# Dilated attention on one core: another order of the steps on TensorE, ScalarE and VectorE, and the maximum's high part on VectorE

## The chip, the cores and the metric

The kernel runs on one core of one Trainium2 chip, as one launch. The metric is the device time of that launch in microseconds (us). A core has five engines that run their own queues of instructions and meet at semaphores: TensorE (PE in the profile; its weight loads are PEld), VectorE (DVE), ScalarE (ACT), GpSimd (POOL) and SyncE (SP), which here issues most transfers.

## The reference

Four stages, each followed by a layer norm of the sum with its input: dilated attention, a mixture of 8 experts, linear attention, and a soft mixture with slots. Only the first is touched:

```python
D_MODEL, NUM_HEADS, HEAD_DIM, DILATION, SEGMENT = 256, 16, 16, 2, 256    # x is (4, 1024, 256)
xs = x[:, global_idx, :]                       # every second row of each segment of 256: 128 rows
qh = xs.reshape(b, n_seg, k, NUM_HEADS, HEAD_DIM)
scores = jnp.einsum('bsqhd,bskhd->bshqk', qh, qh) * scale
attn = jax.nn.softmax(scores, axis=-1)
seg_out = jnp.einsum('bshqk,bskhd->bsqhd', attn, qh)
a_denoms = a_os.sum(axis=-1)                   # and each row is scaled by den / den before it is added
x = _layernorm(x + _L0_attn_ref(x), axis=-1)
```

Queries, keys and values are the same rows. There are 16 segments (4 batches of 1024 rows), each with 16 heads.

## The kernel before

`dilated_attention` (line 176) works through the 16 segments in two steps each, 8 heads a step, 32 steps in all. In the code `p` is the number of the step (a "pair" of its own in the names), `half = p % 2`, and `q` the parity of the segment; all tiles come in twos. A step's work is spread over later steps by lags (`pair(i, k, lag)`, `segment(i, k, lag)`): a function that is called with lag 1 in step p works on step p - 1. In this text a step is even or odd by p, and an even and an odd one are a pair of steps, one segment. `steps` unrolls eight steps at the start and the last ones, and runs the rest in a loop of four (there waits and addresses come from registers).

The way of one step's heads:

- GpSimd, `masks` (line 273): `xmh` and `xml`, the transposed segment times the head mask, high and low part. For an even step it first waits for `xT_ready` and `xl_ready` of the segment; for each it waits for the score two steps back. Behind the odd one it does two small subtractions `w_lo` for the experts' weights (`low_slice`, line 866).
- TensorE, `score` (line 303): six products into `psS`; it waits for the masks and for the exponential two steps back, which frees `psS`.
- VectorE, `maximum` (line 464), the row maximum over 128 keys.
- ScalarE, `high` (line 390): minus the maximum, rounded to the short format, into `negmax`; VectorE, `low` (line 482): what is left of it.
- TensorE, `turn_max` (line 315), lag 1: transposes `negmax` into `psM`. VectorE, `spread` (line 473), lag 1: two copies of it times 0 or 1 (the parities) into `shift`. TensorE, `add_max` (line 326), lag 1: adds it to the score through the `pick` matrices.
- ScalarE, `exponent` (line 400), lag 1, and TensorE, `gather` (line 344), lag 2: probabilities times the values `xaug`.
- Once a segment, in odd steps: ScalarE `keep_out` (line 409), TensorE `turn_out` (line 356), VectorE `divide` (lines 493, 496) and `total` (506, 525, 509: a sum, the statistics of the odd rows, a reciprocal). In even steps: VectorE `finish` (519, called alpha below, and 522) and `sum_up` (525).
- The next segment: TensorE `turn_x` (363) transposes it, ScalarE `keep_x` (421) keeps the high part, VectorE `rest_x` (454) the low part, ScalarE `augment` (414) fills `xaug`. ScalarE also makes the high part of the experts' weights (`high_slice`, 858).

Each engine's order inside a step is written out in its function `step`; nothing else sets it. The lines that give what waits for what, at the change:

```python
wait(pe, xm_ready, p * 2 + 2); wait(pe, prob_ready, p - 1)                                # score(p)
wait(pe, negmax_ready, p + 1); wait(pe, shift_ready, p)                                   # turn_max(p), lag 1
wait(dve, scored, p + 1); wait(dve, hi_ready, p - 1); wait(dve, negmax_ready, p - 1)      # maximum(p)
wait(dve, max_turned, p + 1); wait(dve, shifted, p - 1)                                   # spread(p), lag 1
wait(dve, hi_ready, p + 1)                                                                # low(p)
act.wait_ge(loaded, loads * 16); wait(act, out_raw, seg * 2 - 2)                          # augment(seg)
```

When the 32 steps are through, all engines meet, and the stage of routing starts with the statistics of all rows.

## Time and profile before

| what | value |
|---|---|
| median of 3 runs | 1467.04 us (1466.63 to 1467.55) |
| profiled execution | 1466.65 us, its span 1464.9 us |
| busy in the span: TensorE, weight loads | 1346.3 us (92%), 1207.5 (82%) |
| VectorE, ScalarE, GpSimd | 892.5 (61%), 653.4 (45%), 748.2 (51%) |
| attention, 0 to 134.9 us: its 32 maxima | first at 8.8 us, last at 123.7 us |

Shares over the whole span mix nine stages with different limits; what a change in one of them is worth is read from that stretch alone, by the timeline of each engine. A time in brackets behind an instruction is how long its engine had been idle, and who ended that. Times within the span are from its start.

### The profile page before, as it was taken

The page shows a single profiled execution, that of the slowest core. Times are in us where ns is not written, and L with a number is a line of the kernel's source. Part 1 is how long each engine was busy: PE and PEld are TensorE (multiplying, and loading weights), DVE is VectorE, ACT ScalarE, POOL GpSimd, SP SyncE. Part 2 cuts the span into 40 slices and gives each one's busy share as a digit, 9 for nine tenths or more (in the row PEclk, how much of TensorE's full clock was granted, in tenths as well). Part 3 has the DMA queues.
Part 4 walks back from the last instruction along what each step waited for, and adds up shares of the span by engine and source line. Part 5 has one row for each costly group of instructions (what it writes and reads, how often), then busy time and mean ns, then how long its engine had stood idle before and what let it go on. Part 6 is the DMA issues. An engine that isn't in the chain of part 4 may idle for free. (4 is left out here: it accounts for less than half of the span.)

```text
span 1464.9 us, 29291 instructions
## 1 busy us (share of the span) xinstructions
PE 1346.3 (92%) x9425; PEld 1207.5 (82%) x9426; DVE 892.5 (61%) x1856; ACT 653.4 (45%) x1174; POOL 748.2 (51%) x695
## 2 busy tenths in 40 slices
PE   6776798999999994999989999999999988999998
PEld 3444687888888883777778999999999978999997
DVE  4898422233323324677578888888888853566656
ACT  3554333233333331666544543543543435555553
POOL 5773197765550003331049887987987957240400
PEclk8998799999999997999999999999999999999999
DMA  4102325232210003210033274474474487465450
GB/s 169 61 30 84 124 70 171 100 143 109 86 60 14 14 15 114 92 58 1 1 116 94 85 196 129 146 197 128 144 200 129 141 257 255 159 216 187 152 204 32
DMA packets 112543, 171.49 MB, mean 117 GB/s; under 512 B 6400, under 2 KB 97664, under 8 KB 106336
## 3 DMA queue, kind: packets, MB, share of 16 engines
q1 hardware_dynamic: 103456, 156.27, 33.2%
q0 software_dynamic: 3408, 9.31, 2.2%
q10 hardware_dynamic: 5616, 5.11, 1.0%
q8 instruction: 35, 0.57, 0.2%
q14 instruction: 28, 0.23, 0.0%
HBM read 115.22 MB, written 55.44 MB: 117 GB/s over the span
## 5 line engine op out<-in xcount | busy, mean ns | idle before, releaser
L2126 PE MATMUL comb_psO<-hand_parts,comb_eh 128*128 (+1 forms) x1024 | 198.8, 292 | 0.0
L1791 ACT ACTIVATE disp_raw<-disp_psL 128x512 f32<-128x512 f32 x128 | 76.6, 598 | 198.7 <-PE disp_psL L1703 112.1
L1104 DVE TENSOR_TENSOR moe_hs<-moe_psH,moe_act_a 128x512 f32<-128x512 f32 x78 | 50.2, 686 | 177.2 <-PE moe_psH L998 140.2
L2126 PEld LDWEIGHTS comb_psO<-hand_parts,comb_eh 128*128 128x128 f32 x1024 | 157.6, 190 | 0.1
L1703 PE MATMUL disp_psL<-disp_ph,hand_xh 128*128 (+1 forms) x512 | 148.0, 289 | 0.8 <-DVE disp_e L1976 0.8
L2245 DVE TENSOR_TENSOR comb_el<-comb_psT,comb_eh 128x512 fp32r<-128x512 f32 x128 | 88.1, 688 | 94.1 <-ACT comb_eh L2160 92.3
L1703 PE MATMUL disp_psL<-disp_ph,hand_xl 128*128 (+1 forms) x512 | 145.1, 283 | 0.0
L1703 PE MATMUL disp_psL<-disp_pl,hand_xh 128*128 (+1 forms) x512 | 145.0, 283 | 0.0
L2126 PE MATMUL comb_psO<-hand_parts,comb_el 128*128 (+1 forms) x512 | 144.7, 283 | 0.0
L1727 PE MATMUL disp_psS<-disp_e,last_x 128*128 128x256 f32 x512 | 133.6, 384 | 4.3 <-POOL disp_e L1885 4.3
L1202 POOL DMA_INDIRECT lin_yg<-sorted_y,table_place x32 | 32.3, 1011 | 190.0 <-POOLq L913 143.3
L998 PE MATMUL moe_psH<-w_hi,moe_xh 128*128 x312 | 125.9, 404 | 2.0 <-issue 1.9
L2160 ACT ACTIVATE comb_eh<-comb_psT 128x512 fp32r<-128x512 f32 x128 | 76.4, 597 | 104.7 <-PE comb_psT L2112 104.7
L998 PE MATMUL moe_psH<-w_hi,moe_xl 128*128 x312 | 122.6, 393 | 0.0
L998 PE MATMUL moe_psH<-w_lo,moe_xh 128*128 x312 | 122.4, 392 | 0.0
L1947 DVE RECIPROCAL disp_rs<-disp_rs 128x256 f32<-128x256 f32 x64 | 111.4, 1741 | 0.0
L1888 POOL TENSOR_TENSOR disp_el<-disp_e,disp_eh 128x512 fp32r<-128x512 f32 x64 | 82.8, 1294 | 49.8 <-ACT disp_eh L1788 49.8
L1113 DVE TENSOR_TENSOR moe_hl<-moe_psHT,moe_hh 128x512 fp32r<-128x512 f32 x78 | 50.4, 686 | 91.2 <-ACT moe_hh L1081 88.3
L1703 PEld LDWEIGHTS disp_psL<-disp_ph,hand_xh 128*128 128x128 f32 x512 | 98.3, 192 | 1.5 <-issue 1.2
L1727 PEld LDWEIGHTS disp_psS<-disp_e,last_x 128*128 128x128 f32 x512 | 89.0, 192 | 11.9 <-POOL disp_e L1885 4.9
L1703 PEld LDWEIGHTS disp_psL<-disp_pl,hand_xh 128*128 128x128 f32 x512 | 98.1, 192 | 0.4
L1703 PEld LDWEIGHTS disp_psL<-disp_ph,hand_xl 128*128 128x128 f32 x512 | 98.1, 192 | 0.0
(295 smaller groups left out, 3894.0 us busy)
## 6 DMA issues: line engine op xcount, KB each, us to landing
logits<-disp_raw SPq DMA_DIRECT2D x64, 512.0 KB, 4.1
hand_e<-logits SPq DMA_DIRECT2D x32, 1024.0 KB, 6.5
w_raw<-in_w SPq DMA_DIRECT2D x8, 2048.0 KB
disp_wt<-in_w_slot SPq DMA_DIRECT2D x16, 1024.0 KB, 10.3
w_raw<-in_w SPq DMA_DIRECT2D x8, 1024.0 KB
slot_y<-disp_slots SPq DMA_DIRECT2D x64, 128.0 KB, 3.2
disp_bt<-in_b_slot SPq DMA_DIRECT2D x15, 512.0 KB, 4.9
comb_y_in<-slot_y SPq DMA_DIRECT2D x3, 2048.0 KB, 10.5
```

The costliest lines, as they stand in the source:

```text
L998: last = nc.tensor.matmul(psH[:, n, :], xpart[:, k, :], wpart[:, bass.ds(b, 1), cols].rearrange("p a f -> p (a f)"), start=first, stop=k = ...
L1104: v.tensor_tensor(hs[:, cols], psH[:, 2 + h, :], act_a[:, cols], ALU.mult).then_inc(hs_ready, 1)
L1113: v.tensor_tensor(hl[:, halves[h], :], psHT[:, halves[h], :], hh[:, halves[h], :].bitcast(F32), ALU.subtract).then_inc(hl_ready, 1)
L1202: nc.gpsimd.indirect_dma_start(yg[:, t, :], None, ys_dram, bass.IndirectOffsetOnAxis(route["place"][:, t:t + 1], 0)).then_inc(gathered[t i ...
L1703: last = nc.tensor.matmul(psL[p][:, b, :], xp[:, kd, t * P:(t + 1) * P], pp[:, half, kd, :].rearrange("p a n -> p (a n)"), start=b % 2 == ...
L1727: last = nc.tensor.matmul(psS[kd][:, b, :], xp[:, row, cols], ep[:, b, :], start=mc == 0 and b % 2 == 1 and a == 0, stop=mc == MC - 1 and ...
L1791: nc.scalar.activation(raw[mc % 4][:, half * 2:half * 2 + 2, :], psL[l_bank[mc]][:, half * 2:half * 2 + 2, :], ACT.Copy).then_inc(copied, 1)
L1888: nc.gpsimd.tensor_tensor(el[mc % 4][:], e[mc % 4][:, 0:SPLIT_B, :], eh[mc % 2][:].bitcast(F32), ALU.subtract).then_inc(part_ready, 1)
L1947: v.reciprocal(rs[mc % 2][:], rs[mc % 2][:]).then_inc(rsum_ready, 1)
L2126: last = nc.tensor.matmul(psO[j % 2][:, 0:D], ep[s % EB][:, i, :], yp[:, bass.ds(odd, 1), ch * D:(ch + 1) * D].rearrange("p a d -> p (a d) ...
L2160: nc.scalar.activation(eh[s % EB][:], psT[s % EB][:], ACT.Copy).then_inc(hi_ready, 1)
L2245: v.tensor_tensor(el[s % EB][:], psT[s % EB][:], eh[s % EB][:].bitcast(F32), ALU.subtract).then_inc(lo_ready, 1)
```

## The change

On TensorE a step did `score`, `turn_max`, `turn_x`, `turn_out`, `add_max`, `gather`; now `turn_x`, `turn_out` and `turn_max` come ahead of `score`, and `add_max` directly behind it. On ScalarE `high` is gone, and `keep_x` and `augment` come ahead of the exponential, `keep_out` behind it. VectorE does `high` with a product by -1.0, and the order of its step is new.

```diff
--- before.py
+++ after.py
@@ -364,12 +364,12 @@
                 last.then_inc(xT_raw, 1)
 
             def step(i, k):
-                score(i, k)
-                turn_max(i, k)
                 at = segment(i, k, -2)
                 if at is not None:
                     turn_x(*at, i + 1 + (k + 2) // 4)
                 turn_out(i, k)
+                turn_max(i, k)
+                score(i, k)
                 add_max(i, k)
                 gather(i, k)
 
@@ -380,16 +380,6 @@
 
         @block.scalar
         def _(act):
-            def high(i, k):
-                at = pair(i, k, 0)
-                if at is None:
-                    return
-                p, half = at
-                wait(act, max_ready, p + 1)
-                wait(act, max_turned, p - 1)
-                nc.scalar.activation(negmax[half][:, :, 0:UH], mx[half][:].rearrange("p (a j) -> p a j", a=HG),
-                                     ACT.Copy, scale=-1.0).then_inc(hi_ready, 1)
-
             def exponent(i, k):
                 at = pair(i, k, 1)
                 if at is None:
@@ -421,15 +411,14 @@
                 nc.scalar.activation(xTh[q][:], psT[:], ACT.Copy).then_inc(xT_ready, 1)
 
             def step(i, k):
-                exponent(i, k)
-                high(i, k)
                 at = segment(i, k, -2)
                 if at is not None:
                     keep_x(*at)
-                keep_out(i, k)
                 at = segment(i, k, -1)
                 if at is not None:
                     augment(*at, i + 1 + (k + 1) // 4)
+                exponent(i, k)
+                keep_out(i, k)
                 at = segment(i, k, 3)
                 if at is not None:
                     weights.high_slice(act, at[0], w0_high)
@@ -472,6 +461,16 @@
                 wait(dve, shifted, p - 1)
                 v.tensor_tensor(shift[half][:], psM[:].unsqueeze(1).to_broadcast([P, 2, P]),
                                 c["parity"][:].unsqueeze(2).to_broadcast([P, 2, P]), ALU.mult).then_inc(shift_ready, 1)
+
+            def high(i, k):
+                at = pair(i, k, 0)
+                if at is None:
+                    return
+                p, half = at
+                wait(dve, max_ready, p + 1)
+                wait(dve, max_turned, p - 1)
+                v.tensor_scalar(negmax[half][:, :, 0:UH], mx[half][:].rearrange("p (a j) -> p a j", a=HG), -1.0, None,
+                                ALU.mult).then_inc(hi_ready, 1)
 
             def low(i, k):
                 at = pair(i, k, 0)
@@ -534,15 +533,16 @@
                 row_stats(seg, 0)
 
             def step(i, k):
-                at = segment(i, k, -1)
+                spread(i, k)
+                divide(i, k)
+                maximum(i, k)
+                high(i, k)
+                low(i, k)
+                at = segment(i, k, -2)
                 if at is not None:
                     rest_x(*at)
-                spread(i, k)
-                maximum(i, k)
-                divide(i, k)
+                total(i, k)
                 finish(i, k)
-                low(i, k)
-                total(i, k)
                 sum_up(i, k)
 
             rest_x(0, 0)
```

Line numbers below are each file's own. VectorE, at the end of the eight unrolled steps: step 6 and the beginning of step 7, from `rest_x` on, before (`att_negmax<-att_mx,att_negmax` is `low`, `att_xTl` `rest_x`, `first_x` with two operands `finish`):

```order
L473 TENSOR_TENSOR att_shift<-att_psM,const_parity 128x256 [waits att_shifted,att_max_turned]
L464 TENSOR_REDUCE att_mx<-att_psS 128x8 [waits att_negmax_ready,att_hi_ready,att_scored]
L519 TENSOR_TENSOR att_small<-att_small 128x1 [waits att_fin]
L522 SCALAR_TENSOR_TENSOR first_x<-att_heads,att_small,first_x 128x256 [waits att_aug_ready,att_fin]
L482 SCALAR_TENSOR_TENSOR att_negmax<-att_mx,att_negmax 128x2x4 [waits att_hi_ready]
L525 BN_STATS first_stats<-first_x 128x6 [waits att_fin]
L454 TENSOR_TENSOR att_xTl<-att_psT,att_xTh 128x256 [waits att_xT_ready]
L473 TENSOR_TENSOR att_shift<-att_psM,const_parity 128x256 [waits att_shifted,att_max_turned]
L464 TENSOR_REDUCE att_mx<-att_psS 128x8 [waits att_negmax_ready,att_hi_ready,att_scored]
L493 RECIPROCAL att_rden<-att_psO 128x16 [waits att_out_turned]
L496 TENSOR_TENSOR att_heads<-att_psO,att_rden 128x256 [waits att_heads_ready]
```

and now; step 7 begins with the second `spread`:

```order
L462 TENSOR_TENSOR att_shift<-att_psM,const_parity 128x256 [waits att_shifted,att_max_turned]
L453 TENSOR_REDUCE att_mx<-att_psS 128x8 [waits att_negmax_ready,att_hi_ready,att_scored]
L472 TENSOR_SCALAR att_negmax<-att_mx 128x2x4 [waits att_max_turned,att_max_ready]
L481 SCALAR_TENSOR_TENSOR att_negmax<-att_mx,att_negmax 128x2x4 [waits att_hi_ready]
L443 TENSOR_TENSOR att_xTl<-att_psT,att_xTh 128x256 [waits att_xT_ready]
L518 TENSOR_TENSOR att_small<-att_small 128x1 [waits att_fin]
L521 SCALAR_TENSOR_TENSOR first_x<-att_heads,att_small,first_x 128x256 [waits att_aug_ready,att_fin]
L524 BN_STATS first_stats<-first_x 128x6 [waits att_fin]
L462 TENSOR_TENSOR att_shift<-att_psM,const_parity 128x256 [waits att_shifted,att_max_turned]
L492 RECIPROCAL att_rden<-att_psO 128x16 [waits att_out_turned]
L495 TENSOR_TENSOR att_heads<-att_psO,att_rden 128x256 [waits att_heads_ready]
L453 TENSOR_REDUCE att_mx<-att_psS 128x8 [waits att_negmax_ready,att_hi_ready,att_scored]
```

A new instruction, `high` (L472), stands between the maximum and `low`, and waits for the maximum directly ahead of it; `rest_x` and `finish` now come behind `low`, and the statistics directly behind `finish`; the reciprocal and the heads have moved ahead of the maximum.

TensorE, in the same even step, before (`att_psM` is the turn of the maximum, `att_shift,const_pick` the product with the parities):

```order
L303 MATMUL att_psS<-att_xmh,att_xTh 128x512 [waits att_prob_ready,att_xm_ready]
L303 MATMUL att_psS<-att_xmh,att_xTh 128x512
L303 MATMUL att_psS<-att_xmh,att_xTl 128x512 x2
L303 MATMUL att_psS<-att_xml,att_xTh 128x512 x2
L315 MATMUL att_psM<-const_ident,att_negmax 128x128 [waits att_shift_ready,att_negmax_ready]
L363 MATMUL att_psT<-const_ident,att_xe 128x128 [waits att_xl_ready,att_even_loaded0]
L363 MATMUL att_psT<-const_ident,att_xe 128x128
L326 MATMUL att_psS<-att_shift,const_pick 128x256 [waits att_shift_ready]
L326 MATMUL att_psS<-att_shift,const_pick 128x256 x3
L344 MATMUL att_psOT<-att_prob,att_xaug 32x128 [waits att_outT_ready,att_aug_ready,att_prob_ready]
```

and now:

```order
L363 MATMUL att_psT<-const_ident,att_xe 128x128 [waits att_xl_ready,att_even_loaded0]
L363 MATMUL att_psT<-const_ident,att_xe 128x128
L315 MATMUL att_psM<-const_ident,att_negmax 128x128 [waits att_shift_ready,att_negmax_ready]
L303 MATMUL att_psS<-att_xmh,att_xTh 128x512 [waits att_prob_ready,att_xm_ready]
L303 MATMUL att_psS<-att_xmh,att_xTh 128x512
L303 MATMUL att_psS<-att_xmh,att_xTl 128x512 x2
L303 MATMUL att_psS<-att_xml,att_xTh 128x512 x2
L326 MATMUL att_psS<-att_shift,const_pick 128x256 [waits att_shift_ready]
L326 MATMUL att_psS<-att_shift,const_pick 128x256 x3
L344 MATMUL att_psOT<-att_prob,att_xaug 32x128 [waits att_outT_ready,att_aug_ready,att_prob_ready]
L344 MATMUL att_psOT<-att_prob,att_xaug 32x128 x7
```

The turns now stand ahead of the score, and the six products of the score between the turn of the maximum and the product with the parities.

ScalarE, an odd step, before:

```order
L400 ACTIVATE att_prob<-att_psS 128x1024 [waits att_out_raw,att_shifted]
L390 ACTIVATE att_negmax<-att_mx 128x2x4 [waits att_max_turned,att_max_ready]
L409 ACTIVATE att_outT<-att_psOT 128x512 [waits att_out_raw]
L414 ACTIVATE att_xaug<-first_x 128x16x16 [waits att_out_raw,att_loaded]
L858 ACTIVATE w_hi<-w_raw 128x256 [waits w_loaded1]
L858 ACTIVATE w_hi<-w_raw 128x128 [waits w_loaded2]
```

and now:

```order
L404 ACTIVATE att_xaug<-first_x 128x16x16 [waits att_out_raw,att_loaded]
L390 ACTIVATE att_prob<-att_psS 128x1024 [waits att_out_raw,att_shifted]
L399 ACTIVATE att_outT<-att_psOT 128x512 [waits att_out_raw]
L858 ACTIVATE w_hi<-w_raw 128x256 [waits w_loaded1]
L858 ACTIVATE w_hi<-w_raw 128x128 [waits w_loaded2]
```

The small copy into `att_negmax` is gone, and the copy into `att_xaug`, with its wait for the gather (`att_out_raw`), stands ahead of the exponential.

## Rows read from the trace of the kernel before

**Rows 1.** windows, one stretch of the stage: busy us (instructions) per engine, clock, DMA, GB/s

```profile
60.00:80.00 20.00, 14.50 (x170) 8.73 (x160) 18.11 (x44) 11.25 (x27) 14.15 (x17) 1.00 0.14 46
```

**Rows 2.** timeline of TensorE, one step: start us, us, engine, line; score, turn, picks, gather

```profile
75.45 0.50 PE L303 MATMUL att_psS<-att_xmh,att_xTh 64*128 64x512 f32 x2 [0.64 <-ACT att_prob L400]
...
76.34 0.33 PE L315 MATMUL att_psM<-const_ident,att_negmax 128*128 128x128 f32 x1
...
77.38 0.50 PE L326 MATMUL att_psS<-att_shift,const_pick 64*128 64x256 f32 x4 [0.43 <-DVE att_shift L473]
77.81 0.64 PE L344 MATMUL att_psOT<-att_prob,att_xaug 128*32 128x128 f32 x16
```

**Rows 3.** timeline of ScalarE: a copy into xaug, and an exponential

```profile
75.78 0.42 ACT L414 ACTIVATE att_xaug<-first_x 128x256 f32 x1
...
77.92 1.02 ACT L400 ACTIVATE att_prob<-att_psS 128x1024 f32<-128x1024 f32 x1 [1.23 <-PE att_psS L326]
```

**Rows 4.** timeline of VectorE, one pair of steps, with nothing left out

```profile
73.60 1.21 DVE L464 TENSOR_REDUCE att_mx<-att_psS 128x8 f32<-128x1024 f32 x1
74.73 0.25 DVE L493 RECIPROCAL att_rden<-att_psO 128x16 f32<-128x16 f32 x1
75.12 0.42 DVE L496 TENSOR_TENSOR att_heads<-att_psO,att_rden 128x256 f32<-128x256 f32 x1
75.46 0.82 DVE L482 SCALAR_TENSOR_TENSOR att_negmax<-att_mx,att_negmax 128x8 fp32r<-128x8 f32 x1
76.20 0.40 DVE L506 TENSOR_REDUCE att_small<-att_heads 128x1 f32<-128x256 f32 x1
76.53 0.41 DVE L525 BATCH_NORM_STATS2 first_stats<-first_x  x1
76.87 0.14 DVE L509 RECIPROCAL att_small<-att_small 128x1 f32<-128x1 f32 x1
76.93 0.40 DVE L473 TENSOR_TENSOR att_shift<-att_psM,const_parity 128x256 fp32r<-128x256 f32 x1
77.25 1.20 DVE L464 TENSOR_REDUCE att_mx<-att_psS 128x8 f32<-128x1024 f32 x1
78.38 0.14 DVE L519 TENSOR_TENSOR att_small<-att_small 128x1 f32<-128x1 f32 x1
78.69 0.48 DVE L522 SCALAR_TENSOR_TENSOR first_x<-att_heads,att_small,first_x 128x256 f32 x1 [0.17 <-DVE att_small L519]
79.09 0.16 DVE L482 SCALAR_TENSOR_TENSOR att_negmax<-att_mx,att_negmax 128x8 fp32r<-128x8 f32 x1
79.32 0.43 DVE L525 BATCH_NORM_STATS2 first_stats<-first_x  x1
79.67 0.41 DVE L454 TENSOR_TENSOR att_xTl<-att_psT,att_xTh 128x256 fp32r<-128x256 f32 x1
80.35 0.42 DVE L473 TENSOR_TENSOR att_shift<-att_psM,const_parity 128x256 fp32r<-128x256 f32 x1 [0.28 <-PE att_psM L315]
```

**Rows 5.** timeline of VectorE: the maximum six pairs after the first of rows 4

```profile
116.75 1.21 DVE L464 TENSOR_REDUCE att_mx<-att_psS 128x8 f32<-128x1024 f32 x1
```

**Rows 6.** timeline of GpSimd over the same pair

```profile
75.22 1.04 POOL L273 TENSOR_TENSOR att_xmh<-att_xTh,const_headmask 128x512 fp32r<-128x512 f32 x1
...
77.22 1.15 POOL L866 TENSOR_TENSOR w_lo<-w_raw,w_hi  x2
80.32 1.04 POOL L273 TENSOR_TENSOR att_xmh<-att_xTh,const_headmask 128x512 fp32r<-128x512 f32 x1 [1.96 <-DVE att_xTl L454]
```

**Rows 7.** view of lines 482 and 519: durations in ns, least/median/most, first and last start

```profile
L482 DVE SCALAR_TENSOR_TENSOR att_negmax<-att_mx,att_negmax x32: 157/168/842, 10.3 to 125.5; 128x8 fp32r<-128x8 f32 x32
...
L519 DVE TENSOR_TENSOR att_small<-att_small x16: 140/147/650, 35.2 to 133.8; 128x1 f32<-128x1 f32 x16
```

**Rows 8.** view of line 52: VectorE's small product with a constant, same columns

```profile
L52 DVE TENSOR_SCALAR lin_tmp<-lin_tmp x8: 162/165/380, 583.8 to 736.3; 128x8 f32<-128x8 f32 x8
```

**Rows 9.** timeline of TensorE in the third step: it waits for a load

```profile
17.27 0.69 PE L363 MATMUL att_psT<-const_ident,att_xe 128*128 128x128 f32 x2 [2.44 <-DMA att_xe<-in_x]
```

## The prediction

> **What bounds the kernel now.** I first read the windows over the attention stage, because everything that is changed lies in it. In a steady stretch of 20 us TensorE works 14.5 us, ScalarE 11.3, GpSimd 14.2 and VectorE 18.1, at a granted clock of 1.00 (2.4 GHz) [rows 1]. So this stage is not TensorE's, though the page gives it 92% of the whole span; VectorE has 9% left. The reader should see the second number in that line, not the first: what VectorE is given or spared here comes close to counting in full.
>
> The timeline of VectorE gives the pace. From the maximum at 73.60 to the one six segments later, at 116.75, are 43.15 us, so two steps (one segment, called a pair of steps here) take 7.19 us [rows 4, 5]. Then I followed one turn of the loop. TensorE's score takes 0.89 us until the turn of the maximum behind it starts, the turn 0.33, VectorE's product with the parities (`spread`) 0.42, the product with the picks 0.50, and the exponential 1.02, after which the next score may start [rows 2 to 4]: about 3.4 us a step with the gaps, and nothing of it overlaps. This is the second limit, and the change is aimed at it, since it puts the score between `turn_max` and `add_max`.
>
> The timeline of VectorE over one pair shows how near the two limits lie [rows 4]. From maximum to maximum it takes 7.09 us. In it are two losses: `low` at 75.46 takes 0.82 us instead of 0.16, and behind `rest_x` (79.67) `spread` starts 0.68 later instead of some 0.34, waiting for TensorE. Without the two the same instructions would take 6.1 us. An instruction that needs nothing of the one ahead starts about 0.08 before that one ends (75.12 + 0.42 = 75.54, next at 75.46); one that needs it starts 0.14 to 0.17 behind its end (74.98 to 75.12; 78.52 to 78.69).
>
> The 0.82 is no work. GpSimd's mask product runs from 75.22 to 76.26, and `low` ends at 76.28 [rows 4, 6]; at 79.09 GpSimd is idle and `low` takes 0.16. Line 519, with 128x1 elements, also takes 0.14 or 0.65 [rows 7]. Both read two operands from SBUF, and they wait until the GpSimd instruction under way ends.
>
> **The change part by part.** *ScalarE.* Its copy `high` goes, the rest is put around the exponential. ScalarE is idle before the exponential as it is (1.23 us, [rows 3]), so the copy's absence is worth nothing by itself. In odd steps `augment` now stands ahead of the exponential and waits for the gather of the step, which TensorE issues behind the product with the picks. That holds the exponential by the gather's 0.65 and the copy's 0.42, about 1.0 us [rows 2, 3]. Its reader is the score two steps on, which comes only after VectorE's next `low`. On the scale used below, `spread` starts at 1.89, the picks run from 2.36 to 2.86, the gather to 3.45, the copy to 3.9, the exponential to 4.9; `low` ends at 4.76, and the turn leaves TensorE to the score at 5.0. Cost nothing, while VectorE is the slower one; uncovered, it would cost whatever exceeds that 0.1.
>
> *TensorE.* The score takes the place of the wait for `spread`. Turn, score and picks add up to the same work. What is new is that the turn of pair p stands ahead of score p + 1, so the loop is now score, maximum, `high`, `low`, turn: 0.95 + 0.04 + 1.21 + 0.14 + 0.17 + 0.14 + 0.16 + 0.05 + 0.17, about 3.0 us a step instead of 3.4. That is the intended gain, 0.8 us a pair, if VectorE could follow.
>
> *VectorE.* It gets `high` twice a pair, and three places where an instruction now needs the one directly ahead: maximum to `high`, `high` to `low` (twice each), and `finish` to the statistics, where `low` stood between (78.69, 79.09, 79.32). `high` as such is not in the trace. The nearest row is a product of 128x8 with a constant, 0.165 us, at most 0.38 [rows 8]; I take 0.17, the usual one. Start to start, by the timeline over one pair [rows 4], counted from the start of an even step's `low`: `low` 0.23, `rest_x` 0.35, alpha 0.31, `finish` 0.48 + 0.17, statistics 0.35, `spread` 0.32, reciprocal 0.39, heads 0.34, maximum 1.21 + 0.14, `high` 0.17 + 0.14: 4.60 us to the odd `low`. From there `low` 0.23, sum 0.33, statistics 0.34, reciprocal 0.06, `spread` 0.32 make 1.28, but the score of the next pair ends only 1.37 behind that `low` (0.16 + 0.05 + 0.17 + 0.95 + 0.04); then 1.35 and 0.31: 3.03 us. The pair takes **7.63 us** before any wait for GpSimd, 0.44 more than now. VectorE's own queue, not TensorE's loop, sets it.
>
> *The wait for GpSimd.* Where does it fall next? GpSimd starts the first mask of a segment 0.24 behind the end of `rest_x` (79.67 + 0.41 = 80.08, to 80.32), then four masks 1.00 apart (two from 75.22 to 77.22) and the two `w_lo` pieces of 1.15 together [rows 4, 6]. On the scale above that is 0.88 to 6.03. `finish`, with two SBUF operands, wants to start at 0.89: a dead heat. If it loses, it is held to about 1.78, by 0.9 us. `high` of the odd step stands at 4.29, in the fourth mask, and `low` right behind it, so that one wait may be followed by another: 4.29 becomes 4.78, and `low` then falls into the `w_lo` pieces; about 0.8 together. With `finish` late as well, both fall into `w_lo` and cost 0.4. So the pair takes 7.63 + 0.8 = 8.43, or 7.63 + 1.3 = 8.93. The trace does not decide the dead heat; I take the middle, 8.68, 1.49 above today's 7.19.
>
> The Trainium skill, "SBUF — State Buffer", section Who interferes with whom, says that a VectorE instruction with two SBUF inputs, or a tensor_scalar in a two-port mode, is fully blocked by a GpSimd instruction that reads SBUF. By that rule `high` is exposed itself. Were it not, `low` behind it would meet the same mask, and the sum would be 0.2 to 0.5 a pair lower.
>
> *The beginning.* In the third step TensorE waits until 17.27 for a load [rows 9]. Now the turn and the score stand behind that wait, ahead of the picks: 0.89 + 0.33 = 1.2 us at 2.4 GHz [rows 2], and more here, where two transposes take 0.69; I bound it by 2.0. Steps 2 to 5 carry none of the divisions and sums, so there the shorter loop may give back up to 0.4 a step and more. Between -1.5 and +2 I take +1.
>
> **Sum.** All of `finish`, `divide` and `total` is present from step 6 to 31, 13 pairs. The last has no masks beside it: 12 x 1.49 + 0.44 + 1 = 19.3 us. Nothing behind the stage can absorb it, since routing begins with the statistics of the last segment. The profiled execution took 1466.65 us (span 1464.9); with 19.3 that is 1485.95, I say **1486**. The median of the runs, 1467.04, is 0.4 above that execution, well within what can be told (about 0.2%, 2.9 us).
>
> **The rivals.** *No wait for GpSimd lasts.* The phases shift by themselves until nothing collides, and only the 0.44 is left: 13 x 0.44 + 1 = 6.7, so 1473; with the beginning at its best 1470. For it: GpSimd is idle for a quarter of the pair. Against: the masks start off `rest_x`, so their place in VectorE's order is fixed, not drifting. 0.16; about an eighth of that is within 0.2%.
>
> *Faster, by the shorter loop.* The price is the gap of 0.14 behind which a dependent instruction starts. If `high`, `low` and the statistics follow as early as independent ones, five gaps of 0.23 go: 7.63 - 1.15 = 6.5, with one short wait for GpSimd 6.9. That is 13 x 0.3 = 3.9 below, 1462.8; it decides from 7.0 us a pair down. For it: TensorE's loop of 3.0 allows it, and the 0.66 and 0.34 of today may go. Against: the timeline shows 0.14 and 0.17 in every such place [rows 4]. 0.17, half of it (7.0 to 7.4 a pair) within 0.2%.
>
> The Trainium skill, "VectorE: DVE Perf Modes", section The DRAIN you can't avoid, says that a semaphore after each instruction costs nothing extra. By that rule this rival, at 1462.8, would be the forecast; the trace's 0.14 and 0.17 behind a needed result, against 0.08 ahead of an end, do not agree.
>
> *Worse than the forecast.* `finish`, `high` and `low` each lose nearly a whole mask: 2.3 a pair, 12 x 2.3 = 28, 1494. I count it as the upper end of the forecast.
>
> **Chances.** Forecast (8.1 to 9.5 a pair) 0.67, no lasting wait 0.16, faster rival 0.17. Faster by over 0.2%: 0.09. Within: 0.08 + 0.02 = 0.10. Slower: 0.67 + 0.14 = 0.81. The range runs from the rival without waits, 1470, to 1494; it leaves out the faster rival.
>
> **What would show it.** Right: maxima of segments some 8.4 to 8.9 us apart; `high` and `low` of odd steps with durations far over 0.17, beside masks or `w_lo`; those of even steps near 0.17; line 521 over 0.48 in part of the steps; VectorE without idle time on TensorE except before the maxima of even steps; TensorE's score directly behind the turn. Wrong: a pair under 7.4, dependent starts within 0.05 of the end ahead, or TensorE idle behind the exponential.

## The result, and the profile of the changed kernel

The changed kernel takes 1479.52 us (median of 5 runs, 1477.92 to 1483.09) against 1467.04 for the kernel before (5 runs, 1460.73 to 1470.15). The ratio of runs is 1.0096, with a 95% interval of 1.0067 to 1.0125: slower by some 12.5 us, where 19 were forecast, and inside the range of 1470 to 1494.

All of it arises in the attention stage. Routing begins with its first statistics, which read the last segment; the view of the tile `route_mean` (duration in ns, least/median/most, then first and last start in us) gives that start, for the kernel before and then for the changed one:

```profile
L47 DVE TENSOR_TENSOR route_mean<-first_stats x1: 215/215/215, 135.3 to 135.3; 128x32 f32<-128x32 f32 x1
```

```profile
L47 DVE TENSOR_TENSOR route_mean<-first_stats x1: 217/217/217, 151.2 to 151.2; 128x32 f32<-128x32 f32 x1
```

That is 15.9 us later. The two spans (1464.9 and 1477.8) lie 12.9 apart, so 3 us come back afterwards. Single totals of the kernel before spread over 12 us (17 further runs: 1456.49 to 1468.73), therefore this start is the measure for the experiments, called "the statistics" from here on. Each of them has one trace, and how far the start varies from one execution of a kernel to the next was not measured, so differences of some tenths of a microsecond carry nothing.

The windows over the stretch of [rows 1], now. VectorE has fallen from 18.1 to 16.1 us of work in 20, TensorE has risen from 14.5 to 15.2 although it does fewer products (131 against 170), and the granted clock is 0.80:

```profile
60.00:80.00 20.00, 15.20 (x131) 9.61 (x131) 16.14 (x39) 7.28 (x15) 11.89 (x14) 0.80 0.12 39
```

In windows of 3 us (columns as before: length, busy time of TensorE, its weight loads, VectorE, ScalarE and GpSimd, clock, DMA, GB/s) the clock is 1.00, 0.91 and 0.50, so it steps between 2.4 and 1.2 GHz:

```profile
66.00:69.00 3.00, 2.67 (x33) 1.87 (x35) 2.42 (x8) 2.01 (x5) 1.15 (x2) 1.00 0.09 30
69.00:72.00 3.00, 1.41 (x10) 0.74 (x8) 2.64 (x6) 0.00 (x0) 2.90 (x3) 0.91 0.00 0
72.00:75.00 3.00, 2.42 (x23) 1.34 (x23) 2.68 (x8) 1.71 (x4) 1.32 (x2) 0.50 0.00 0
```

VectorE's timeline over one pair of steps, from maximum to maximum, answers to [rows 4]; it takes 8.21 us:

```profile
63.75 1.22 DVE L453 TENSOR_REDUCE att_mx<-att_psS 128x8 f32<-128x1024 f32 x1
65.00 0.17 DVE L472 TENSOR_SCALAR att_negmax<-att_mx 128x8 fp32r<-128x8 f32 x1
65.20 0.17 DVE L481 SCALAR_TENSOR_TENSOR att_negmax<-att_mx,att_negmax 128x8 fp32r<-128x8 f32 x1
65.30 0.42 DVE L505 TENSOR_REDUCE att_small<-att_heads 128x1 f32<-128x256 f32 x1
...
66.03 0.40 DVE L462 TENSOR_TENSOR att_shift<-att_psM,const_parity 128x256 fp32r<-128x256 f32 x1
66.87 1.23 DVE L453 TENSOR_REDUCE att_mx<-att_psS 128x8 f32<-128x1024 f32 x1 [0.44 <-PE att_psS L303]
68.13 0.17 DVE L472 TENSOR_SCALAR att_negmax<-att_mx 128x8 fp32r<-128x8 f32 x1
68.34 0.17 DVE L481 SCALAR_TENSOR_TENSOR att_negmax<-att_mx,att_negmax 128x8 fp32r<-128x8 f32 x1
68.44 0.42 DVE L443 TENSOR_TENSOR att_xTl<-att_psT,att_xTh 128x256 fp32r<-128x256 f32 x1
68.78 0.15 DVE L518 TENSOR_TENSOR att_small<-att_small 128x1 f32<-128x1 f32 x1
69.08 1.34 DVE L521 SCALAR_TENSOR_TENSOR first_x<-att_heads,att_small,first_x 128x256 f32 x1 [0.16 <-DVE att_small L518]
70.56 0.43 DVE L524 BATCH_NORM_STATS2 first_stats<-first_x  x1
70.91 0.41 DVE L462 TENSOR_TENSOR att_shift<-att_psM,const_parity 128x256 fp32r<-128x256 f32 x1
...
71.96 1.21 DVE L453 TENSOR_REDUCE att_mx<-att_psS 128x8 f32<-128x1024 f32 x1
...
76.60 1.22 DVE L453 TENSOR_REDUCE att_mx<-att_psS 128x8 f32<-128x1024 f32 x1 [1.75 <-PE att_psS L303]
```

Three things are to be seen. `high` and `low` take 0.17 each and follow 0.03 behind the end of what they need. `finish` takes 1.34 where it works 0.48. And before the maximum of the even step VectorE waits for TensorE, 0.44 here (at 66.87) and 1.75 ten microseconds later. GpSimd's timeline (which answers to [rows 6]) shows what `finish` met, a mask that began 0.02 behind it:

```profile
69.10 1.04 POOL L273 TENSOR_TENSOR att_xmh<-att_xTh,const_headmask 128x512 fp32r<-128x512 f32 x1 [1.04 <-DVE att_xTl L443]
70.10 1.22 POOL L273 TENSOR_TENSOR att_xml<-att_xTl,const_headmask 128x512 fp32r<-128x512 f32 x1
...
72.28 1.03 POOL L273 TENSOR_TENSOR att_xml<-att_xTl,const_headmask 128x512 fp32r<-128x512 f32 x1
75.82 1.14 POOL L866 TENSOR_TENSOR w_lo<-w_raw,w_hi  x2 [2.50 <-ACT w_hi L858]
```

The view of `finish` gives it for all 16 executions, 484 ns free, 1208 or 1342 held; the view of the maximum gives the waits:

```profile
L521 DVE SCALAR_TENSOR_TENSOR first_x<-att_heads,att_small,first_x x16: 484/1208/1342, 35.1 to 149.9; 128x256 f32 x10, 128x256 f32<-128x256 f32 x6
```

```profile
L453 DVE TENSOR_REDUCE att_mx<-att_psS x32: 1211/1224/1226, 8.7 to 140.5; 128x8 f32<-128x1024 f32 x32
its engine sat idle before it (us, times) until:
  PE att_psS L303: 18.4, 18
```

TensorE's timeline tells where the 1.75 comes from. It stood idle for 1.59 us, since `spread` waited behind the held `finish`; then come the products at the lower clock (the gather takes 1.08, 0.64 in [rows 2]) and a score that waited for an exponential, and takes 1.65 until it ends instead of 0.9:

```profile
71.37 0.74 PE L326 MATMUL att_psS<-att_shift,const_pick 64*128 64x256 f32 x4 [1.59 <-DVE att_shift L462]
72.04 1.08 PE L344 MATMUL att_psOT<-att_prob,att_xaug 128*32 128x128 f32 x16
73.05 0.69 PE L363 MATMUL att_psT<-const_ident,att_xe 128*128 128x128 f32 x2
73.71 0.47 PE L315 MATMUL att_psM<-const_ident,att_negmax 128*128 128x128 f32 x1
74.76 0.80 PE L303 MATMUL att_psS<-att_xmh,att_xTh 64*128 64x512 f32 x2 [0.58 <-ACT att_prob L390]
75.32 0.66 PE L303 MATMUL att_psS<-att_xmh,att_xTl 64*128 64x512 f32 x2
75.75 0.66 PE L303 MATMUL att_psS<-att_xml,att_xTh 64*128 64x512 f32 x2
```

Over nine steady pairs the maxima run from 46.15 to 125.67, 8.84 us a pair; before, the same nine took 44.61 to 109.66, 7.23 a pair. These pairs hold 14.5 of the 15.9 us, the steps ahead of them 1.5 (the steps behind them give back 0.1).

### The profile page after: what moved, and what is told of

It reads as the page before. It is cut to its first block and busy times, and to the rows that moved or that the text cites. A ratio compares the mean times of both kernels' runs of the same rounds, so it can differ in the third digit from the quotient of the medians.

```text
span 1477.8 us, 29305 instructions
## 1 busy us (share of the span) xinstructions
PE 1353.4 (92%) x9425; PEld 1214.6 (82%) x9426; DVE 906.0 (61%) x1888; ACT 650.2 (44%) x1142; POOL 749.7 (51%) x695
## 6 DMA issues: line engine op xcount, KB each, us to landing
w_raw<-in_w SPq DMA_DIRECT2D x8, 1024.0 KB, 10.4
```

## The experiments

The table puts them side by side: the statistics' start; the mean pair over the same nine; by how much `high`, `low` and `finish` lasted longer than 0.17, 0.17 and 0.48, over all their executions (excesses of under 0.05 left out); what VectorE waited for the score ahead of the maxima within the nine pairs; the granted clock from 40 to 120 us; the total of the profiled execution. The totals come from several chips and stand here for completeness: the kernel before took 1468.42 us on the chip of e1 to e4, 1462.93 on that of e5 to e8, and 1463.41 (median of 17) on that of e9 to e12.

| kernel | statistics | pair | `high` | `low` | `finish` | waits | clock | total |
|---|---|---|---|---|---|---|---|---|
| before | 135.3 | 7.23 | - | 8.7 | 0.2 | 0 | 1.00 | 1466.65 |
| changed | 151.2 | 8.84 | 1.2 | 3.9 | 8.7 | 8.7 | 0.82 | 1479.52 |
| e1 | 150.6 | 8.50 | 1.2 | 3.9 | 8.1 | 5.7 | 0.82 | 1476.81 |
| e2 | 158.4 | 9.14 | 7.1 | 10.7 | 0.2 | 7.2 | 0.81 | 1482.99 |
| e3 | 158.1 | 9.14 | 7.1 | 10.7 | 0.2 | 7.2 | 0.81 | 1488.12 |
| e4 | 153.3 | 8.63 | 10.4 | 6.3 | 0.5 | 0 | 0.82 | 1479.12 |
| e5 | 139.3 | 7.69 | - | 9.2 | 0.5 | 6.1 | 0.94 | 1465.38 |
| e6 | 130.2 | 6.98 | - | 0 | 0.5 | 3.5 | 1.00 | 1457.42 |
| e7 | 134.3 | 7.48 | 0 | 0 | 0.7 | 3.4 | 0.96 | 1463.57 |
| e8 | 132.8 | 7.24 | 0 | 0 | 0.5 | 4.1 | 1.00 | 1458.13 |
| e9 | 149.1 | 8.77 | 0 | 0 | 8.7 | 8.1 | 0.85 | 1477.96 |
| e10 | 154.8 | 8.85 | 8.1 | 11.7 | 0.7 | 5.8 | 0.83 | 1481.72 |
| e12 | 135.7 | 7.31 | 0 | 0 | 0.2 | 4.0 | 0.98 | 1460.53 |
| e11 | 134.5 | 7.40 | - | 0 | 0.2 | 0 | 1.00 | 1460.1 |

**Parts undone.** e1 undoes one step of ScalarE's new order: `exponent` and `keep_out` come ahead of `augment` again. (In this fence and the next the lines that fetch `at` are left out.)

```diff
-                augment(*at, i + 1 + (k + 1) // 4)
-                exponent(i, k)
-                keep_out(i, k)
+                exponent(i, k)
+                keep_out(i, k)
+                augment(*at, i + 1 + (k + 1) // 4)
```

> The changed kernel with one step of ScalarE's order undone: augment stands behind the exponential and keep_out again. Measure: the start of the first statistics instruction of routing (line 47), 135.3 us before and 151.2 in the changed kernel. Theory A (finish waits for the masks, some 0.8 us in 12 steps): that wait stays, line 521 keeps its median of 1.21 us, and the attention stage shrinks by less than 3 us, to 148 or more. Theory B (the exponential behind augment and the gather makes the next score late, and TensorE falls to 1.2 GHz in between): the waits of 1.7 us before every fourth maximum go, the granted clock stays at 1.00, and the stage ends 8 to 10 us earlier, at 141 to 143.

Measured: the statistics at 150.6, 0.6 us earlier, as theory A had it. In the nine pairs the waits for the score fall from 8.7 to 5.7 us, which is a third of a microsecond a pair; the beginning loses most of it again (step 9 at 48.21, not 46.15). `finish` is held as before. So the copy ahead of the exponential does cost a little in the loop, but it is not where the 15.9 us went.

e2 moves `rest_x`, whose end starts the masks, to the end of VectorE's step, and e3 does both.

```diff
-                rest_x(*at)
                 total(i, k)
                 finish(i, k)
                 sum_up(i, k)
+                rest_x(*at)
```

> The changed kernel with rest_x as the last of VectorE's even step instead of directly behind low: the masks then start after finish and the statistics. Theory A: line 521 falls from 1.21 to 0.48 us in all steps, 12 x 0.75 = 9 us, less what high and low of the odd step now lose to the masks, which come about 1.3 us later (up to 0.8 a segment): stage end at 142 if nothing collides again, 147 to 151 if high and low take the wait over. Theory B: little moves, 149 to 151, since the score's wait for the exponential is untouched.

> Both edits of the two runs before in one kernel. If the two losses are separate, their gains add: theory A and B together give 151.2 - 9 - 9 = 133, at or below the 135.3 of the kernel before. If one covers the other, it ends where the better single edit ends. VectorE's own queue, with gaps of 0.03 us as the changed kernel's trace shows them, would bound it at about 7.1 us a pair, the 7.19 of before.

Measured: `finish` is free, and `high` and `low` pay instead, 17.8 us together, so the statistics come at 158, later than either theory had them (147 to 151 if `high` and `low` took the wait over), and far from the 133 that e3 would have shown had the losses been separate. Two rows of e2's VectorE show `low` held behind a free `high`:

```profile
75.83 0.17 DVE L472 TENSOR_SCALAR att_negmax<-att_mx 128x8 fp32r<-128x8 f32 x1
76.03 0.89 DVE L481 SCALAR_TENSOR_TENSOR att_negmax<-att_mx,att_negmax 128x8 fp32r<-128x8 f32 x1
```

The loss moves with the order, it does not go. e3 agrees with e2 to 0.3 us in the statistics, so with `high` and `low` held, ScalarE's order decides nothing that can be told.

**Parts alone.** e4 is the kernel before with `high` on VectorE directly ahead of `low`, and nothing reordered (the body of `high` moves as in the change).

```diff
 # ScalarE
                 exponent(i, k)
-                high(i, k)
 # VectorE
+                high(i, k)
                 low(i, k)
```

> The kernel before with one part of the change alone: high on VectorE, directly ahead of low, no order changed. Theory C (the added instruction is the price, because VectorE is the bound): 28 steps of full load x about 0.2 us = 4 to 6 us, stage end at 139 to 141. If the price is in the order: within 1.5 us of 135.3; a gain of up to 1 us is possible, as low no longer waits for ScalarE behind the exponential.

Measured: 153.3, which no theory had foreseen (the highest expectation was 139 to 141). `high`, with one operand in SBUF and a constant, is held just like `low`: 14 times, 10.4 us in all, and from 20 to 40 us the granted clock is 0.50 (0.80 before). `high` and `low` together are held by 8 us more than `low` alone was. The table's column of waits does not show the rest, as it falls ahead of `spread`, not of the maximum: there VectorE waits 16.9 us for TensorE's turn, against 9.1 before. This single move makes the kernel before as slow in this stage as the whole change does. How much of it is the holding and how much the lower clock, which the holding may or may not have caused, one trace does not separate.

e5 is the kernel before with TensorE's new order alone.

```diff
-                score(i, k)
-                turn_max(i, k)
                 ...
                 turn_out(i, k)
+                turn_max(i, k)
+                score(i, k)
                 add_max(i, k)
```

> The kernel before with TensorE's order alone changed (turns ahead of the score); high stays on ScalarE, and VectorE's order stays. Theory A (VectorE with its waits for GpSimd is the bound, TensorE's loop is not): low keeps its wait of 0.66 us a segment, and the maximum can no longer start early, so the pair of steps stays at 7.1 to 7.6 us and the statistics of routing start within 4 us of 135.3. The rival (TensorE's loop was the bound and the new order is worth 0.4 us a step): 135.3 - 13 x 0.5 = 129 or less. A third: the clock falls to 1.2 GHz in part of the stage, as in the kernel with high on VectorE alone; then 140 to 150 with a granted clock of 0.8.

Measured: 139.3, a pair at 7.69, at the edge of theory A. TensorE's order by itself does not help: `low`, held by 9.2 us, now stands ahead of the turn and the score, and the score ahead of the next maximum (waits of 6.1 us that were not there before).

**The cause taken away.** The next three runs test whether `high` and `low` are held because they read the maxima from SBUF while GpSimd runs. e6 is e5 with the two buffers of maxima in PSUM, in the bank of the turned maximum; with TensorE's old order the turn could write that bank while VectorE writes a maximum there, so it was not tried with that order. e7 is the same edit to e3, and e8 is e6 with `high` on VectorE.

```diff
-        mx = [m.sb(f"mx{i}", [P, PH]) for i in range(2)]
-        psM = m.ps("psM", [P, P])
+        maxima = m.ps("psM", [P, P + 2 * PH])
+        psM = maxima[:, 0:P]
+        mx = [maxima[:, P + i * PH:P + (i + 1) * PH] for i in range(2)]
```

> The run before (TensorE's order alone) and the maxima in PSUM instead of SBUF, in psM's bank behind its 128 columns; with TensorE's new order nobody else uses that bank between the maximum and low. low then reads one operand from SBUF instead of two. Theory A: low takes 0.16 to 0.25 us in every step, its 8.6 us of waiting go, VectorE needs 6.3 us a pair and waits little: a pair of 6.5 to 6.8, stage end 13 x 0.5 = 6 us or more ahead of the kernel before, at 125 to 130. Theory of the clock alone: what counts is whether TensorE stays at 2.4 GHz, and low's wait is incidental; then it ends where the run before ends, within 2 us.

> The changed kernel with rest_x behind finish and augment behind the exponential (the third run, 158.1 us to routing) and the maxima in PSUM, so that high and low can't be held by GpSimd, and finish comes ahead of the masks. Theory A: high 0.17 to 0.25 and low 0.17 to 0.25 us throughout, all 18 us of waiting for GpSimd gone; VectorE's own 7.05 us a pair and about 0.3 for TensorE give 7.4, stage end at 137 to 141, the clock back at 1.00. Rival (the falling clock has another cause than VectorE's waits for GpSimd): clock at 0.8 and a stage end over 148.

> As e6 (TensorE's order, maxima in PSUM, VectorE's old order), and high on VectorE directly ahead of low instead of on ScalarE. It measures the price of the added instruction with no wait for GpSimd in the way: high takes 0.17 to 0.25 us and 0.03 to 0.1 behind it, 32 times. If VectorE is the bound: 13 pairs x 0.4 to 0.6 = 5 to 8 us more than e6. If TensorE's loop is: at most 2 us more, or less, as low no longer waits for ScalarE behind the exponential.

Measured: not one `high` or `low` is held in any of the three, so it is reading the maxima from SBUF that exposes them. Against the kernels without that edit the statistics come 9.1 us (e5 to e6) and 23.8 us (e3 to e7) earlier, where 9.2 and 17.8 us of holding went. e6 starts routing at 130.2, 5.1 us ahead of the kernel before; with `high` on VectorE (e8) it is 2.6 later, the price of the added instruction where nothing holds it. Of the expectations, e6 came out at the edge (125 to 130, with a pair of 6.5 to 6.8, was said), e7 better than said (137 to 141), and e8's 2.6 between its two theories. The Trainium skill, "SBUF — State Buffer", section Who interferes with whom, says that a VectorE instruction with at most one SBUF input does not contend with GpSimd, two-port modes aside. The runs agree: `low` with its maxima in PSUM takes 165 to 167 ns in all 32 executions of e9, 166 to 961 with both inputs in SBUF (e10).

**The changed kernel, mended in two steps.** e9 is the changed kernel with its maxima in PSUM; e10 has only `rest_x` behind `finish`; e12 has both.

> The changed kernel with one edit: the 128x8 maxima are kept in PSUM, beside the turned maximum, instead of SBUF. My theory (each small VectorE instruction that reads SBUF alone is held by whatever GpSimd instruction runs when it comes up, and in the changed kernel that is `finish`, which keeps its SBUF operands): `finish` stays held, 8 to 9 us in all, in ten or more of its executions, the pair of steps stays at 8.2 to 8.9 us, and only what `high` and `low` lose (1.23 + 3.90 us) comes back: routing's first statistics start at 144 to 148 us (changed kernel 151.2). Rival (it is the maxima in SBUF that cost, as the 9.1 us between e5 and e6 and the 23.8 us between e3 and e7 suggest): statistics at 140 us or earlier, pair at 7.5.

Measured: 149.1, a pair at 8.77 (144 to 148 had been expected; the rival wanted 140 or less). `high` and `low` are free, `finish` is held by 8.7 us as before, and the statistics gain 2.1 of the 5.1 us that `high` and `low` had been held. VectorE and GpSimd in e9, the dead heat once more, by 0.02 us:

```profile
85.99 1.34 DVE L522 SCALAR_TENSOR_TENSOR first_x<-att_heads,att_small,first_x 128x256 f32 x1 [0.16 <-DVE att_small L519]
```

```profile
86.01 1.04 POOL L274 TENSOR_TENSOR att_xmh<-att_xTh,const_headmask 128x512 fp32r<-128x512 f32 x1 [1.73 <-DVE att_xTl L444]
```

> The changed kernel with one edit: in VectorE's step `rest_x` stands behind `finish` and no longer ahead of it, so the masks that GpSimd starts at the end of `rest_x` begin when `finish` is over. My theory (the loss moves on to the next small instruction that meets a mask): line 521 at 0.48 us in nearly all executions, and in its place `high` and `low` of the odd steps held, 8 us or more together; routing's first statistics at 148 to 156 us (changed kernel 151.2). Rival (the masks, 0.6 us later, miss `high` and `low` as they mostly do in the changed kernel): statistics at 138 to 143 us, pair of steps at 7.5 to 8.0 us.

Measured: 154.8, as my theory had it. `finish` is free, and in its place both small instructions of the odd step are held, one after the other:

```profile
75.73 0.76 DVE L472 TENSOR_SCALAR att_negmax<-att_mx 128x8 fp32r<-128x8 f32 x1
76.52 0.96 DVE L481 SCALAR_TENSOR_TENSOR att_negmax<-att_mx,att_negmax 128x8 fp32r<-128x8 f32 x1
```

> The changed kernel with both edits: `rest_x` behind `finish`, and the maxima in PSUM. My theory: no small VectorE instruction is left that meets a mask with SBUF operands alone, so `high`, `low` and `finish` all take their own 0.17, 0.17 and 0.48 us, the pair of steps takes 7.2 to 7.5 us, the granted clock stays at 0.9 to 1.0, and routing's first statistics start at 132 to 137 us, as in e7 (134.3), although ScalarE's order is the changed one; total 1460 to 1466. Rival (ScalarE's copy of `augment` ahead of the exponential costs as well, since the loop is now short enough to need it): 1 us a pair more, statistics at 140 to 146 us, with VectorE idle for TensorE's score ahead of each second maximum.

Measured: 135.7, a pair at 7.31, clock 0.98, and in the loop nothing is held. With both edits the changed kernel is back at the kernel before (135.3), although ScalarE's order is the changed one. The two edits gain 2.1 and -3.6 us singly and 15.5 together: the first leaves `finish` where the masks meet it, the second frees `finish` and puts `high` and `low` in the masks' way. From e9 to e12 8.5 us of holding go, and 13.4 us of time; of the other 4.9, 4.1 are waits for the score (8.1 to 4.0 in the nine pairs). They go together with the held `finish` and with the clock, which rises from 0.85 to 0.98.

**A faster kernel?** e11 is e6 with `low` between the reciprocal and the product of `divide`, and between the two halves of `finish`.

```diff
                 v.reciprocal(rden[q]...)
+                low(i, k)
                 v.tensor_tensor(heads[q]...)
...
                 v.tensor_tensor(alpha, den, rec, ALU.mult)
+                low(i, k)
                 v.scalar_tensor_tensor(row, heads[q][:], alpha, row, ...)
...
-                low(i, k)
+                if segment(i, k, 5) is None and segment(i, k, 6) is None:
+                    low(i, k)
```

> The kernel before with TensorE's new order and the maxima in PSUM (this is e6, statistics at 130.2 us, pair 6.98 us) and one edit more: `low` stands between the reciprocal and the product of `divide`, and between the two halves of `finish`, in place of the 0.13 to 0.26 us that VectorE waits there for its own last result. My theory (VectorE's own queue bounds e6): 0.15 us less at each of the two gaps and 0.1 to 0.2 us less in front of each maximum, because the turn and the score start 0.4 us earlier; pair of steps 6.4 to 6.6 us, statistics at 124 to 127 us, whole kernel 1450 to 1454 us, ratio to the kernel before 0.988 to 0.991. Rival (ScalarE's `high`, which stands behind the exponential, is not ready, and `low` waits where it now stands): pair 6.9 to 7.1 us, statistics at 129 to 132 us, ratio 0.992 to 0.996, with VectorE idle on ScalarE ahead of `low`.

Measured: 134.5, pair 7.40, no theory's number, but the rival's sign: VectorE idles on ScalarE's `high` ahead of `low`.

```profile
74.53 0.17 DVE L483 SCALAR_TENSOR_TENSOR att_negmax<-att_psM,att_negmax 128x8 fp32r<-128x8 f32 x1 [0.43 <-ACT att_negmax L391]
...
78.05 0.17 DVE L483 SCALAR_TENSOR_TENSOR att_negmax<-att_psM,att_negmax 128x8 fp32r<-128x8 f32 x1 [0.53 <-ACT att_negmax L391]
```

`high` stands behind the exponential there, and VectorE, which in e6 did the heads or `finish` meanwhile, now stands still. e11 is worse than e6 in this stage by 4.3 us. Over several runs it takes 1461.3 us (12 runs) against 1463.41 (17 runs) for the kernel before, ratio 0.998, interval 0.9964 to 0.9996: 0.2%, no more than can be told. e6 has a single run (1457.42, with the kernel before at 1462.93 on the same chip); that it would beat both kernels over several runs is likely from its statistics at 130.2, and not shown.

## Why the prediction was right, and where it was not

The side and the place were right, and the size of 19 us came out at 12.5 by errors that in part cancelled: of the terms in the sum, one was right, three were too high, and one was missing.

*`finish` loses a dead heat with the mask (0.9 a pair, weighed by a half).* Right in mechanism and price: held by 0.73 to 0.86 us, in all 10 of its executions in the loop. It was no toss-up; the mask and `finish` both follow `rest_x` at a fixed distance, so they meet alike each time. e10 and e12 confirm the cause.

*`high` and `low` of the odd step in the masks or `w_lo` (0.4 to 0.8 a pair).* Wrong for the loop of the changed kernel: 0.17 us each there. With `finish` late, GpSimd's last mask ends at 73.31, just as `high` comes up (73.20), and GpSimd then waits 2.50 us for ScalarE's `w_hi`; `high` and `low` fall in that gap (in the first case of the prediction, with `finish` early, they are held, as e10 shows). In the loop of the changed kernel neither is held in any step; what the table has for them falls in steps 1 to 7 and 29. That `high` is exposed itself, which the prediction took from a rule, e4 and e10 show: 10.4 and 8.1 us.

*VectorE's own queue, 7.63 a pair.* Too high. Of the 8.84 us, `finish` loses 0.8 and the score 0.97 (8.74 in nine pairs), which leaves 7.07. The term that was mis-sized is the gap of 0.14 behind a needed result: between maximum, `high` and `low` it is 0.03, four times a pair, which is 0.44 of the 0.56. (The sum also has the turn of the maximum at 0.17, where [rows 2] shows 0.33; in the changed kernel the score starts 0.25 behind the turn.)

The traces tell what the 0.14 was. The rows that the prediction read it from lie in the rolled loop. In the unrolled steps of the same kernel before, `divide`'s product follows its reciprocal by 0.04 (38.93 to 38.97), and in the changed kernel `finish` follows alpha by 0.03:

```profile
38.69 0.24 DVE L493 RECIPROCAL att_rden<-att_psO 128x16 f32<-128x16 f32 x1
38.97 0.42 DVE L496 TENSOR_TENSOR att_heads<-att_psO,att_rden 128x256 f32<-128x256 f32 x1
```

```profile
34.93 0.15 DVE L518 TENSOR_TENSOR att_small<-att_small 128x1 f32<-128x1 f32 x1
35.11 0.48 DVE L521 SCALAR_TENSOR_TENSOR first_x<-att_heads,att_small,first_x 128x256 f32<-128x256 f32 x1
```

In the loop a register instruction of VectorE's sequencer stands at these places. Before `finish` there is one in each of the ten executions of the loop, and in none of the unrolled ones (durations in ns):

```profile
L521 DVEq FUSED_REGOPS  x10: 64/73/89, 43.3 to 122.7; - x10
```

So the 0.14 to 0.27 are a gap of 0.03 to 0.04, the register instructions, and the start behind them. Between maximum, `high` and `low` no such instruction stands, in the loop either, and the gap is 0.03 everywhere. The prediction took what the loop's register instructions cost for the price of waiting for a result.

*TensorE hides behind VectorE, and ScalarE's copy costs nothing.* Wrong, and this term was missing: 0.97 us a pair of waiting for the score. The forecast counted TensorE at 2.4 GHz; it ran at 0.82 of that. e1 puts a third of the waits (0.34 a pair) on ScalarE's order. The rest shrinks when `finish` is freed (e9 to e12), and the clock rises with it; how the rest divides between the later start of `spread` and the lower clock is not shown. The nine pairs thus give 8.84 where 8.68 stood in the sum, which is luck: a queue taken too long by 0.56 and waits for GpSimd too long by 0.25 (1.05 in the middle of the two cases, 0.8 measured), against 0.97 that was left out.

*Twelve pairs and a beginning of +1.* The beginning gave +1.5. The full price falls on nine pairs, not twelve: up to step 9 the changed kernel loses 1.5 in all (it is 2.2 ahead at step 5), and behind step 27 the two keep step (from there to routing 25.5 us now, 25.6 before). 9 x 1.61 + 1.5 - 0.1 = 15.9, against 19.3 forecast.

*Nothing behind the stage absorbs it.* Here 3 us came back. From 230 to 280 us, in the experts, the clock was 0.90 in the trace before and 1.00 in the changed one; the windows of before, then of the changed kernel:

```profile
230.00:280.00 50.00, 44.46 (x244) 38.41 (x243) 12.92 (x22) 13.49 (x26) 35.64 (x20) 0.90 0.45 140
```

```profile
230.00:280.00 50.00, 45.39 (x281) 40.22 (x280) 14.54 (x25) 15.47 (x30) 38.86 (x34) 1.00 0.46 138
```

The 3 us need not belong to the change. From the statistics to the end, where all kernels here have the same code, the traces of e1 to e12 take 1322.8 to 1328.3 us; the changed kernel takes 1326.6, within that, and the kernel before 1329.6, just above. In e11 and e12 the same 50 us show a clock of 0.93, and their rest is among the shortest (1323.9 and 1323.0), so that clock does not explain it either.

*The rivals.* The faster one needed early dependent starts, and between maximum, `high` and `low` it had them (0.03). It still fell, because the price that it left out, one short wait for GpSimd, was 0.8 each pair and brought TensorE's with it. With both freed in e12 the pair takes 7.31, against 7.23 before, so even then it would have been no gain. "Phases shift until nothing collides" is refuted by ten equal holds in ten. The Trainium skill, "VectorE: DVE Perf Modes", section The DRAIN you can't avoid, has it that a semaphore after each of eight copies costs nothing extra. No run here leaves a semaphore out, so that is not tested. The traces have 0.03 to 0.04 behind a needed result wherever no register instruction stands between, and the 0.14 that the prediction held against that rule came with such an instruction.

## What to carry to other kernels

Beside a GpSimd engine that works 14 us in 20, a small VectorE instruction in SBUF costs not its 0.17 us but up to a whole GpSimd instruction, and each reordering tried here (e2, e3, e10) moved this wait instead of ending it: look for the operand that can live in PSUM first, and reorder then. When a wait falls on an instruction that the next TensorE product needs, price it at more than its length: here 8.5 us of holding were 13.4 us of time. Before an instruction is moved from an idle engine to the busy one, count what it is exposed to there. And when a gap between two instructions is read as a price, look whether the engine's sequencer did something in it, and read the same pair in an unrolled step.

## What the runs showed of the hardware

- A product of 128x8 with a constant, one operand in SBUF, is held by GpSimd as one with two operands is: 0.69 to 1.07 us where it works 0.17 (e2 to e4 and e10). The holding goes both ways: the second mask behind the start of a held `finish` takes 1.22 us instead of 1.04 (at 70.10), ten times in the changed kernel and ten in e9, and never in e12.
- An instruction that needs the result directly ahead of it started 0.03 to 0.04 us behind its end. Where a register instruction of the sequencer stood between them, as it does in the rolled loop ahead of the heads, `finish` and the statistics, it was 0.13 to 0.17, and 0.25 to 0.27 with two of them.
- The granted clock of TensorE in the stage (40 to 120 us) was 0.94 to 1.00 in every kernel whose pair took under 7.7 us, and 0.81 to 0.85 in every one over 8.4. What TensorE's idle times say about it is not clear-cut. Those over 0.3 us between its products sum to 20 us before, 20 in the changed kernel, 18 in e6, 19 in e12 and 15 in e4, with clocks of 1.00, 0.82, 1.00, 0.98 and 0.82. Single ones over 1.2 us are 0, 7, 0, 0 and 0 of them; e5, at 0.94, has 7. So neither their sum nor their length sorts the kernels: e4 has none over 1.02 us in this stretch and the low clock all the same, and from 20 to 40 us, with TensorE busy 18.5 us of 20, its clock was 0.50. What decides it stays open.
